# Cross-attention with adaptive layer norm on Trainium2: weights normalised and turned one step behind their exponential, output projection three steps behind, rows turned into a second bank of the attention output

## What is computed

```python
def _L0_xcond_ref(x_q, x_kv, t_vec, Wq, bq, Wkv, bkv, Wp, bp, Wss_q, bss_q, Wss_kv, bss_kv):
    ...
        h = (x - mu) / jnp.sqrt(var + EPS)
        ss = jax.nn.silu(c) @ W_ss + b_ss
        scale, bias = jnp.split(ss, 2, axis=-1)
        return (1.0 + scale)[:, None, :] * h + bias[:, None, :]
    ...
    xq = _ada_ln(x_q, t_vec, Wss_q, bss_q)
    xkv = _ada_ln(x_kv, t_vec, Wss_kv, bss_kv)
    q = (xq @ Wq + bq).reshape(B, Lq, nh, dh)
    kv = (xkv @ Wkv + bkv).reshape(B, Lkv, 2, nh, dh)
    k = kv[:, :, 0]
    v = kv[:, :, 1]
    scores = jnp.einsum('bqhd,bkhd->bhqk', q, k) / jnp.sqrt(jnp.float32(dh))
    attn = jax.nn.softmax(scores, axis=-1)
    out = jnp.einsum('bhqk,bkhd->bqhd', attn, v).reshape(B, Lq, H)
    return x_q + (out @ Wp + bp)
```

## Time and profile before

| | |
|---|---|
| median of 3 runs | 1246.71 us (1243.78 to 1247.53) |
| the profiled execution | 1245.6 us |
| its span in the trace | 1243.7 us |
| PE busy | 1167.9 us, 94% of the span |
| DVE busy | 1045.9 us, 84% |
| POOL busy | 947.6 us, 76% |
| ACT busy | 891.2 us, 72% |
| TensorE clock granted | full speed (2.4 GHz) from 150 to 1100 us |

### The profile page before, as it was taken

How to read it: one execution, slowest core, us unless ns; L and a number is a source line. 1 busy time by engine, 2 the same in 40 slices (tenths; PEclk the granted TensorE clock), 3 DMA queues, 4 the chain that set the end, 5 groups by cost and what they waited for, 6 DMA issues and landing times.

```text
span 1243.7 us, 33482 instructions
## 1 busy us (share of the span) xinstructions
PE 1167.9 (94%) x11072; PEld 691.2 (56%) x11072; DVE 1045.9 (84%) x1797; ACT 891.2 (72%) x1688; POOL 947.6 (76%) x1202
## 2 busy tenths in 40 slices
PE   7788899999999999999999999999999999999976
PEld 2564455555555555555555555555555555555543
DVE  4744889888988898888989889889889898898985
ACT  2466777787777877787777777776878777777633
POOL 2543687979798888979797988889796978888443
PEclk9798899999999999999999999999999999999998
DMA  9110132222322322223222232222322222222111
GB/s 331 51 43 26 52 103 84 97 99 79 101 84 93 101 76 101 89 88 101 83 94 100 77 101 83 94 101 76 101 83 94 101 79 98 88 89 84 60 60 52
DMA packets 59865, 111.91 MB, mean 90 GB/s; under 512 B 6412, under 2 KB 6440, under 8 KB 59832
## 3 DMA queue, kind: packets, MB, share of 16 engines
q1 hardware_dynamic: 41400, 77.92, 18.1%
q10 hardware_dynamic: 18432, 33.56, 8.7%
HBM read 77.90 MB, written 33.55 MB: 90 GB/s over the span
## 4 chain that ended last, share of the span: by engine, by line
POOL 49%; issue 35%; PE 3%; POOLq 2%; DVE 1%; ACT 1%; ACTq 0%; DVEq 0%
POOL xr L414 11%; POOL half_den L421 9%; POOL xh L381 6%; POOL w_lo L428 5%; POOL veps L367 5%; POOL xr L390 4%; POOL rstd L369 4%; POOL var L365 2%; POOLq L224 2%; POOL neg_mean L356 1%; PE ps_o L1196 1%; PE ps_q L1131 0%; POOL w_tmp L404 0%; PE ps_o L1131 0%; PE ps_t L1165 0%
## 5 line engine op out<-in xcount | busy, mean ns | idle before, releaser
L615 ACT ACTIVATE pr<-pr,exp_scale 128x1024 f32<-128x1024 f32 x128 | 147.3, 1150 | 101.4 <-DVE pr L895 101.4
L421 POOL TENSOR_TENSOR half_den<-pr 128x512 f32<-128x512 f32 x128 | 162.7, 1271 | 71.5 <-ACT pr L615 71.2
L875 DVE SCALAR_TENSOR_TENSOR pr<-pr,rden 128x512 f32<-128x512 f32 x256 | 172.5, 714 | 4.3
L390 POOL TENSOR_TENSOR xr<-xr,bp_row 128x512 f32<-128x512 f32 x128 | 162.4, 1269 | 13.2 <-POOL rstd L369 6.9
L564 ACT ACTIVATE q_hi<-ps_q,cur_bq 128x512 f16<-128x512 f32 x126 | 86.3, 685 | 119.3 <-PE ps_q L1131 118.9
L414 POOL TENSOR_TENSOR xr<-y,xr 128x512 f32<-128x512 f32 x128 | 162.9, 1272 | 10.2 <-ACT y L530 10.2
L1165 PE MATMUL ps_t<-ident,pr 128*128 128x128 f32 x1024 | 147.6, 280 | 23.5 <-DVE pr L875 23.4
L903 DVE TENSOR_TENSOR pt_lo<-ps_t,pt_hi 128x512 f16<-128x512 f32 x256 | 163.3, 678 | 1.4 <-ACT pt_hi L554 1.4
L883 DVE TENSOR_REDUCE mx<-ps_s 128x8 f32<-128x512 f32 x256 | 163.8, 680 | 0.0
L895 DVE TENSOR_TENSOR pr<-ps_s,mx 128x512 f32<-128x512 f32 x256 | 163.3, 678 | 0.0
L845 DVE TENSOR_TENSOR xT_lo<-ps_t,xT_hi 128x512 f16<-128x512 f32 x128 | 88.5, 691 | 86.5 <-ACT xT_hi L505 86.5
(11 more groups left out here) (163 smaller groups left out, 2429.2 us busy)
## 6 DMA issues: line engine op xcount, KB each, us to landing
x_in<-in_x_dram SPq DMA_DIRECT2D x128, 256.0 KB, 2.8
xr<-in_x_dram SPq DMA_DIRECT2D x128, 256.0 KB, 2.9
out_dram<-xr ACTq DMA_DIRECT2D x128, 256.0 KB, 2.3
raw<-in_L_xcond_Wss_kv_dram SPq DMA_DIRECT2D x4, 512.0 KB, 5.3
cx<-in_ctx_dram SPq DMA_DIRECT2D x1, 2048.0 KB, 12.1
raw<-in_L_xcond_Wss_q_dram SPq DMA_DIRECT2D x4, 512.0 KB, 13.0
raw<-in_L_xcond_Wkv_dram SPq DMA_DIRECT2D x2, 1024.0 KB, 15.5
wq<-in_L_xcond_Wq_dram SPq DMA_DIRECT2D x1, 1024.0 KB, 16.5
```

Of the source, the lines that this page charges most:

```text
L390: pool.tensor_tensor(xr[:, s, :], xr[:, s, :], bp_row[:, :], ALU.add).then_inc(xr_ready, 1)
L421: pool.tensor_tensor(half_den[:, :, :], pr[:, off % 2, :, 0:LKV // 2], pr[:, off % 2, :, LKV // 2:LKV], ALU.add).then_inc(half_done, 1)
L615: act.activation(pr[:, i % 2], pr[:, i % 2], ACT.Exp, scale=exp_scale[:, 0:1]).then_inc(exp_done, 1)
L875: dve.scalar_tensor_tensor(out=pr[:, off % 2, hs, :], in0=pr[:, off % 2, hs, :], scalar=P_UNIT, in1=rden[:, hs].unsqueeze(2).to_broadcast( ...
```

## The change

On PE, the turn of a unit's weights goes from the middle of a step to its end, and the product with the values and the output projection each come one step later. On DVE the normalisation of the weights goes behind the work on the next unit's scores, and their low part is taken a step later; on ACT the order of the step is new. The rows are turned into the second bank of ps_v in place of the first bank of ps_t (`x_bank`; the first eight units keep ps_t), the attention output uses only the first bank of ps_v, and there is one more drain step. No instruction is added to or taken from a unit's work. POOL keeps its order, with `add_rows` and `residual` one unit further back.

```diff
--- before.py
+++ after.py
@@ -249,8 +249,12 @@
...
                 step(B - 1, i)
-            for i in range(3):
+            for i in range(4):
                 step(B, i)
+
+        def x_bank(b, off):
+
+            return ps_t[:, 0, :] if isinstance(b, int) and unit(b, off) < PER else ps_v[:, 1, :]
 
@@ -443,10 +447,10 @@
...
                 mean(b, i + 8)
-                add_rows(b, i - 3)
+                add_rows(b, i - 4)
                 moments(b, i + 8)
                 await_moments(b, i + 8)
-                residual(b, i - 2)
+                residual(b, i - 3)
                 normalise(b, i + 8)
@@ -502,7 +506,7 @@
...
                     wait(act, q_mm, unit(b, off - 4))
-                act.copy(xT_hi[:, s, :, cols], ps_t[:, 0, :].rearrange("p (k n) -> p k n", k=KC))\
+                act.copy(xT_hi[:, s, :, cols], x_bank(b, off).rearrange("p (k n) -> p k n", k=KC))\
                    .then_inc(xT_hi_done, 1)
@@ -510,7 +514,7 @@
...
                 wait(act, out_mm, unit(b, off))
-                act.copy(oT_hi[:, :, :], ps_v[:, off % 2, :].rearrange("p (k n) -> p k n", k=KC)).then_inc(oT_hi_done, 1)
+                act.copy(oT_hi[:, :, :], ps_v[:, 0, :].rearrange("p (k n) -> p k n", k=KC)).then_inc(oT_hi_done, 1)
 
@@ -589,34 +593,34 @@
...
             def step(b, i):
-                output(b, i - 3)
+                sum_rows(b, i + 8)
+                output(b, i - 4)
                 if not (isinstance(b, int) and b == 0 and i == 0):
                     turned_x(b, i + 7)
-                sum_rows(b, i + 8)
-                turned_o(b, i - 2)
+                turned_o(b, i - 3)
+                turned_p(b, i - 2, 0)
+                turned_p(b, i - 2, 1)
+                sum_squares(b, i + 8)
                 if isinstance(b, int) and b == 0 and i in (0, 1):
...
                     scaled_wq_hi(b + 1, i - 2)
-                if i == 1:
-                    values(b)
                 if i == 4:
                     query_bias(b + 1)
+                if i == 2:
+                    values(b)
+                query(b, i + 4)
                 if i == 7:
                     key_blocks(b + 1)
-                sum_squares(b, i + 8)
-                query(b, i + 4)
-                turned_p(b, i - 1, 0)
-                turned_p(b, i - 1, 1)
                 if exists(b, i):
...
                     act.activation(pr[:, i % 2], pr[:, i % 2], ACT.Exp, scale=exp_scale[:, 0:1]).then_inc(exp_done, 1)
-                if exists(b, i - 3):
-                    s = (i - 3) % 4
-                    wait(act, y_ready, upto(b, i - 3))
-                    act.dma_start(out_units[unit(b, i - 3)], xr[:, s, :]).then_inc(stored[s], 16)
+                if exists(b, i - 4):
+                    s = (i - 4) % 4
+                    wait(act, y_ready, upto(b, i - 4))
+                    act.dma_start(out_units[unit(b, i - 4)], xr[:, s, :]).then_inc(stored[s], 16)
 
@@ -842,14 +846,14 @@
...
                 wait(dve, xT_hi_done, upto(b, off))
-                dve.tensor_tensor(xT_lo[:, s, :, cols], ps_t[:, 0, :].rearrange("p (k n) -> p k n", k=KC),
+                dve.tensor_tensor(xT_lo[:, s, :, cols], x_bank(b, off).rearrange("p (k n) -> p k n", k=KC),
                                   xT_hi[:, s, :, cols], ALU.subtract).then_inc(xT_done, 1)
...
                 wait(dve, oT_hi_done, upto(b, off))
-                dve.tensor_tensor(oT_lo[:, :, :], ps_v[:, off % 2, :].rearrange("p (k n) -> p k n", k=KC),
+                dve.tensor_tensor(oT_lo[:, :, :], ps_v[:, 0, :].rearrange("p (k n) -> p k n", k=KC),
                                   oT_hi[:], ALU.subtract).then_inc(oT_done, 1)
@@ -916,17 +920,17 @@
...
                     turned_x(b, i + 7)
+                turned_o(b, i - 3)
+                score_max(b, i, 0)
+                score_max(b, i, 1)
+                softmax_shift(b, i)
+                turned_p(b, i - 2, 0)
+                turned_p(b, i - 2, 1)
                 weight_sums(b, i - 1)
-                turned_o(b, i - 2)
                 denominators(b, i - 1)
...
                 normalise_p(b, i - 1)
-                score_max(b, i, 0)
-                score_max(b, i, 1)
-                softmax_shift(b, i)
-                turned_p(b, i - 1, 0)
-                turned_p(b, i - 1, 1)
                 query(b, i + 4)
@@ -1109,9 +1113,10 @@
...
                 wait(pe, xT_done, unit(b, off))
-                wait(pe, pt_done, 2 * unit(b, off - 9) + 1)
+                if isinstance(b, int) and unit(b, off) >= PER:
+                    wait(pe, k32_done, CT)
                 for k in range(KC):
-                    last = pe.transpose(ps_t[:, 0, P * k:P * (k + 1)], xh[:, off % 2, P * k:P * (k + 1)], ident[:, :])
+                    last = pe.transpose(x_bank(b, off)[:, P * k:P * (k + 1)], xh[:, off % 2, P * k:P * (k + 1)], ident[:, :])
                 last.then_inc(xT_turned, 1)
@@ -1157,8 +1162,8 @@
...
                     wait(pe, norm_done, 2 * unit(b, off) + h + 1)
-                    if h == 0:
-                        wait(pe, xT_done, upto(b, off + 8))
+                    if h == 0 and isinstance(b, int) and b == 0:
+                        wait(pe, xT_done, PER)
                     wait(pe, pt_done, 2 * unit(b, off - 1) + h + 1)
@@ -1171,14 +1176,16 @@
...
                     return
+                if isinstance(b, int) and b == 0:
+                    wait(pe, k32_done, CT)
                 if off % PER == 0:
                     wait(pe, vb_done, 4 * (b + off // PER + 1))
-                wait(pe, oT_done, unit(b, off - 1))
+                wait(pe, oT_done, unit(b, off))
                 wait(pe, pt_done, 2 * upto(b, off))
...
                         for e in range(2):
-                            last = pe.matmul(ps_v[64 * e:64 * (e + 1), off % 2, P * m:P * (m + 1)],
+                            last = pe.matmul(ps_v[64 * e:64 * (e + 1), 0, P * m:P * (m + 1)],
                                              vb[:, part, 2 * m + e, :, :].rearrange("p h c -> p (h c)"),
@@ -1200,10 +1207,10 @@
...
                 project(b, i + 4)
+                project_out(b, i - 3)
+                turn_x(b, i + 8)
+                weigh(b, i - 2)
                 turn_p(b, i - 1)
-                project_out(b, i - 2)
-                turn_x(b, i + 8)
-                weigh(b, i - 1)
 
```

## The result

The changed kernel takes 1283.51 us (median of 4 runs, 1281.65 to 1283.94), the kernel before 1247.10 us beside it (4 runs, 1243.78 to 1247.53): 1.0295 times as long, 95% interval 1.0274 to 1.0316. The change costs 36 us; 34.5 were forecast. The profiled span grew from 1243.7 to 1279.8 us.

The account below looks back on a forecast made before the run. It took PE's 8.1 us to bound the shortest steps and POOL those that also prepare the next sample's weights. 1245.6 + 37.5 (fifteen samples) - 3 (the last) = 1280 us; range 1238 to 1298.

Parts of the forecast that it names:

- The port: DVE's normalisation, both inputs in SBUF, and POOL's instructions exclude each other; in the drain it waited 0.80 of 0.94 us.
- Rival B: POOL's instruction waits until both normalisation halves are done: slower by less, 1250 to 1268 us; chance 0.16.
- The walk through a sample: Eight step lengths summed from row lengths, with the normalisation meeting POOL's large instructions: 71.3 us against 68.8.
- the term of +2.5 us a sample: Each of fifteen samples takes 2.5 us more, from the eight summed steps: +37.5 us in all.
- POOL's 8.0 us: POOL's own work in a step with weights work, without the 0.8 us lost to DVE's normalisation; 5.8 without weights work.
- PE's 8.1 us that "stays": PE's own work per step, read from the shortest step of 8.10 us, was to be unchanged, as no instruction is added.
- Before the change this costs almost nothing.: In the kernel before, the normalisation meets only POOL's small instructions; POOL loses 0.47 + 0.33 = 0.8 us in the step read.
- The last sample: No rows to normalise; the loop of exponential, sum, normalisation and next maximum is cut: -3 us, between -8 and 0.
- The keys: ACT's 2.53 us key copy, now ahead of step 7's exponential, makes step 0 the longest: 9.8 us against 8.96.
- The waits: PE waits at the turn of the weights for DVE's pair, 40 us or more; DVE's wait for the sum of halves goes.
- Rival A: Decoupling wins, collisions rare or cheap: 66.4 us a sample, end at 1207 us, or 1243 with half the collisions; chance 0.17.
- Rival C: Gains in steps 2 to 5 and losses in 0, 1 and 6 cancel: 1243 to 1250 us; chance 0.06.

## Why the prediction was right, and where its terms were off

The mechanism was right: the pair falls on POOL's large instructions and the port makes the kernel slower. The forecast of 1280 lies 3.5 us under the median. That it comes so near is in part luck, since several terms miss in opposite directions. Its steps:

**The port.** Right, and shown by taking one input out of SBUF. One half of the normalisation was forecast at 1.1 us on average and up to 1.8; it takes 1.19, at most 1.77. Eps and power at 0.19 and 0.55: so. Large POOL instructions of some 1.8: 1.72. The hold ends a little before the POOL instruction does, and POOL slips in between the halves, as one instruction in place of two showed. Rival B, the pair that stays together, is out.

**The walk through a sample** (end of pair to end of pair; the forecast counts from the same point):

| step | 6 | 7 | 0 | 1 | 2 | 3 | 4 | 5 | sum |
|---|---|---|---|---|---|---|---|---|---|
| forecast | 8.3 | 8.2 | 9.8 | 8.9 | 8.7 | 9.1 | 9.1 | 9.2 | 71.3 |
| before | 8.05 | 8.09 | 8.98 | 8.29 | 8.67 | 8.89 | 8.78 | 9.05 | 68.8 |
| measured | 8.60 | 7.65 | 10.58 | 8.86 | 8.50 | 8.84 | 8.77 | 9.00 | 70.8 |

The sum is 0.5 us too high, so the term of +2.5 us a sample measured +2.0. Where the loss lies is off by more: steps 1 to 5 were to lose 1.3 us together and lost 0.3 (43.97 us against 43.68 before), and steps 6, 7 and 0 lost 1.7 where 1.2 were forecast. In steps 3 and 4 POOL had lost 0.8 us to the port before the change and loses 0.78 after it, so that little changes there. Steps 3 and 4 are over by 0.3 each: I charged POOL's 8.0 us with a wait of 0.55 for each half, but the w_lo ahead of the pair waits for nothing, w_tmp loses 0.33 and the sum of halves 0.45. Step 7 runs at DVE's 7.65, not at PE's 8.2: DVE is late by then and waits for nothing in it. Step 0 is 0.78 us longer than forecast, so that the two together miss by 0.2. PE's 8.1 us that "stays" was wrong twice. The shortest steps read on DVE, 8.03 and 8.10 us, are DVE catching up behind a long one; PE's own step was 8.16. And in the new order it is 8.31, which the reciprocal in PSUM uncovered and DVE had hidden.

**"Before the change this costs almost nothing."** Wrong: it cost 31.6 us. Two parts of that were on the page and I priced neither as time. In the loop POOL lost 0.8 us in each heavy step, where it was the bound: 68.8 us a sample became 67.1, about 15 x 1.7 = 25.5 us. And in the last sample the pair of 2.09 us was part of every step: 8.53 us became 7.72, and the last ten steps together 79.8 instead of 87.1 us.

**The last sample.** This term failed, in sign too: forecast -3, between -8 and 0. The prediction took the drain's step of 8.53 us to be a loop that the change cuts. The loop was there, but the port made it what it was (the line above), and the change put two collisions where there was one, as the drain's rows show: steps of 9.4 to 10.5 us, where most took 8.53 before. Only the very last fell, from 9.43 to 6.28. The reciprocal ten steps ahead of the last came at 1172.17 us instead of 1141.37 (+30.8), the last at 1264.56 instead of 1228.47 (+36.1): these steps cost +5.3 us. Here luck helped: the two misses nearly cancel, 14 samples at 0.5 less each are -7, the end is +8.3.

**The keys.** Right in kind: step 0 was forecast as the longest and is, but it grew by 1.6 us where 0.8 were forecast. Moving the copy gives 11.8 us back, 0.8 a sample.

**The waits.** PE was to wait 40 us or more for the pair at the turn; it is 36.0 us (76 times), somewhat under; before it was 23.4. DVE's wait for the sum of halves is gone; it was 0.66 us a step where POOL had weights work, and the freed time went to the pair.

**Rival A.** Its first half happened: POOL left the chain, DVE's wait went. But even with the port out of the way the new order is 3.5 us slower than the old one, not faster, since PE's own 8.31 us is all there is to gain towards.

**Rival C.** Its first half nearly happened: steps 1 to 5 take 0.3 us more than before. Its second, that half of the loss in step 0 stays away, did not.

## What to carry to other kernels

Before an instruction is moved, look not only at who waits for it but at what runs beside it in its new place, and find one row where the two met: here one row of the drain (2.09 us for 1.29) was what set the forecast apart from rival A's. A long DVE instruction with both inputs in SBUF is the thing to look for beside a busy POOL; if one input is small, such as a broadcast reciprocal, put it in PSUM, which here was worth 2.6% of the old kernel and 5% of the new one. An order of steps that cuts one loop is worth only the distance to the next bound, and is to be tried after such collisions are gone.

## What the runs showed of the hardware beyond that

- With rden in PSUM, DVE's 128x512 instruction (two 4-byte inputs, one of them a broadcast) took 683 ns on average, against 677 ns for the shortest with both in SBUF, and no POOL instruction beside it was stretched. The Trainium skill's page "SBUF — State Buffer", section "Who interferes with whom", says that an instruction with at most one SBUF input doesn't contend, outside the modes that use both ports; the runs agree.
- A waiting POOL instruction gets its turn between two DVE instructions that stand back to back, though DVE's second one is ready: it happened to w_tmp in step 3 (721.59 to 722.96). With the rest of a POOL instruction ahead of it and one in between, a pair comes to 3.38 us.
- On PE, one more change of tile shape in a step went with 0.16 us more (8.31 against 8.16). Whether the shape alone is the cause wasn't isolated.
